# Value tiles of the projections made with an image's first two quarters, and stored ahead of its last quarter's parts

## The chip, the cores and the metric

The kernel runs on one core of a Trainium2 chip. The metric is the device time of one execution in microseconds (us). Besides the timed runs there is one execution recorded by the hardware profiler; all rows below come from it, and its times count from the start of its span.

## The reference, cut to what matters

The program is a small vision tower: four images of 512 tokens by 256 channels go through three attention layers with 16 heads of 16 channels, and through two mixture-of-experts layers. The change touches only the projections at the head of each attention layer: from the layer's input they make queries, keys and values.

```python
# layer "tok" (all tokens, no mask)
qkv = einsum('bysd,ed->byse', x, w_qkv) + b_qkv          # q, k, v: 256 columns each
# layer "rot" (rotary positions, causal)
q = x @ wq_w + wq_b; k = x @ wk_w + wk_b; v = x @ wv_w + wv_b
q = apply_rope(q, pos, ROPE_BASE); k = apply_rope(k, pos, ROPE_BASE)
# layer "top" (causal, the 32 largest scores of a row are kept)
q = x @ Wq.T + bq; k = x @ Wk.T + bk; v = x @ Wv.T + bv
```

In "rot" and "top" a class token stands before the 512 tokens, so keys and values have 513 rows.

## The kernel before

The program is a sequence of stages. Each has its own buffers and semaphores and ends in a barrier of all engines, so that nothing of the next stage starts before the last DMA of this one has landed. The three projection stages are calls of one function, `project` (tags "tok", "rot", "top"); the attention stage that follows each one reads queries, keys and values back from DRAM.

`project` goes through the images b = 0 to 3, and in each through four *quarters* k = 0 to 3. Quarters 0 and 1 make the two halves of the channels of the queries, quarters 2 and 3 those of the keys, each as 128 channels by 512 tokens. With each quarter one *value tile* (128 tokens by 256 channels) is made. In a quarter

- TensorE makes the quarter in `ps` (L288; in "rot" also a swapped version in `ps_rot`, L293), then the value tile k in `ps_v` (L298). Both have two buffers. It waits before a quarter until `full` of the quarter two earlier is out of PSUM, and before a value tile until the tile two earlier was added (`v_ok`).
- VectorE adds the bias and scales, into `full` (L365, in "rot" L352, L355 and L360). Then it calls `split` for the quarter *before* this one: `rest` = `full` - `hi` (L330), and the addition of the bias to the value tile of that earlier quarter, from PSUM into the big buffer `va` (L336). The first such addition of a stage also waits for `v_ones`, that is for GpSimd to have filled `va` with zeros and ones (L401, L403).
- ScalarE rounds `full` to bf16 as `hi` (L388), and after it rounds the earlier quarter's `rest` as `mid` (L381). Before `hi` it waits until the stores of the same quarter of the image before have landed (`stored[k]`), since there is one set of parts for each k.
- GpSimd makes `lo` = `rest` - `mid` (L411).
- SyncE waits for `lo` and issues two DMAs of 192 KB for the quarter (L253). After the fourth quarter of an image it waits for its four value tiles and issues one DMA of 1024 KB (L261; in "top" L257, in rows by position). At the end of the stage it waits for all stores (L266 to L268).

All DMAs here are issued by SyncE, on one queue. After the last image VectorE runs `split` once more, for the last quarter. So the end of a stage is a chain: last `full`, `rest` of quarter 2 and of quarter 3, `mid`, `lo`, the stores, the barrier.

Of the kernel before, what the change touches and what calls it, by code (L numbers as in the profile page):

```python
# [24 lines left out]
ALU = mybir.AluOpType  # L25
# [3 lines left out]
P = 128  # L29
B = 4  # L30
S = 512
D = 256
DC = D // P
NH = 16
HD = D // NH
NQ = S // P
NT = B * NQ
G = 4
HG = NH // G
# [148 lines left out]
def project(c, tag, w, qkb, vb, cls, rope=None):  # L188
# [10 lines left out]
    with c.stage() as st:  # L199
        full = c.sbuf(st, f"{tag}_full", [P, 2, S + 1], F32)  # L200
        rest = c.sbuf(st, f"{tag}_rest", [P, 2, S + 1], F32)
        parts = c.sbuf(st, f"{tag}_parts", [P, SPLIT, 4, S + 1], BF16)
        lo, mid, hi = parts[:, 0], parts[:, 1], parts[:, 2]
        kcls = c.sbuf(st, f"{tag}_kcls", [P, DC, B], F32)
        va = c.sbuf(st, f"{tag}_va", [P, NT, NH, STRIP], F32)
# [7 lines left out]
        ps_v = c.psum(st, f"{tag}_ps_v", [P, 2, S])  # L213
# [7 lines left out]
        hi_ok = c.sem(st, f"{tag}_hi_ok")  # L221
        rest_ok = c.sem(st, f"{tag}_rest_ok")
        mid_ok = c.sem(st, f"{tag}_mid_ok")
        lo_ok = c.sem(st, f"{tag}_lo_ok")
        stored = [c.sem(st, f"{tag}_stored{i}") for i in range(4)]
        v_mm = c.sem(st, f"{tag}_v_mm")
        v_ok = c.sem(st, f"{tag}_v_ok")
        v_ones = c.sem(st, f"{tag}_v_ones")
# [9 lines left out]
        def span(k):  # L238
            return slice(0 if cls and k // 2 == 1 else 1, S + 1)

        @block.sync
        def _(sp):
            for i in range(4):
                sp.sem_inc(stored[i], 16)
            for b in range(B):
                for k in range(4):
                    which, gg = k // 2, k % 2
                    dst = (c.qd, c.kd[S + 1 if cls else S])[which]
                    sp.wait_ge(hi_ok, b * 4 + (k + 1))
                    sp.wait_ge(mid_ok, b * 4 + (k + 1))  # L250
                    sp.wait_ge(lo_ok, 2 + b * 4 + (k + 1))
                    for i in range(2):
                        sp.dma_start(dst[b, 2 * gg + i].rearrange("i d h t -> (d h) i t"),  # L253
                                     parts[i * HD * HG:(i + 1) * HD * HG, :, k, span(k)]).then_inc(stored[k], 16)
                sp.wait_ge(v_ok, 2 + (b + 1) * NQ)
                if by_position:
                    sp.dma_start(c.vp[b, 1:, :].rearrange("(n p) w -> p n w", p=P),  # L257
                                 va[:, b * NQ:b * NQ + NQ, :, :].rearrange("p n h s -> p n (h s)")
                                 ).then_inc(v_out, 16)
                else:  # L260
                    sp.dma_start(c.vd[b], va[:, b * NQ:b * NQ + NQ, :, :].rearrange("p n h s -> p n (h s)")  # L261
                                 ).then_inc(v_out, 16)
            if by_position:
                sp.wait_ge(vc_ok, 1)
                sp.dma_start(c.vp[:, 0, :], vc[:, :, :].rearrange("b h s -> b (h s)")).then_inc(v_out, 16)
            sp.wait_ge(v_out, 16 * (B + 1 if by_position else B))  # L266
            for i in range(4):
                sp.wait_ge(stored[i], 16 + B * step_stores)  # L268

        @block.tensor  # L270
        def _(pe):
            pe.wait_ge(c.fetched, fetched)
            if cls:
                for gg in range(DC):
                    for ch in range(DC):
                        pe.matmul(ps_c[:, 0, gg * B:gg * B + B], w[:, ch, D + gg * P:D + gg * P + P],
                                  c.xt[:, ch, :, 0], start=ch == 0, stop=ch == DC - 1)
                for ch in range(DC):
                    mm = pe.matmul(ps_c[0:B, 1, 0:D], c.xt[:, ch, :, 0], w[:, ch, 2 * D:3 * D],
                                   start=ch == 0, stop=ch == DC - 1)  # L280
                mm.then_inc(cls_mm, 1)

            for b in range(B):
                for k in range(4):
                    which, gg = k // 2, k % 2
                    pe.wait_ge(full_ok, b * 4 + (k + 1))
                    for ch in range(DC):
                        mm = pe.matmul(ps[:, k % 2, :], w[:, ch, which * D + gg * P:which * D + gg * P + P],  # L288
                                       c.xt[:, ch, b, 1:S + 1], start=ch == 0, stop=ch == DC - 1)
                    if rope:  # L290
                        at = (3 + which) * D + gg * P
                        for ch in range(DC):
                            mm = pe.matmul(ps_rot[:, k % 2, :], w[:, ch, at:at + P],  # L293
                                           c.xt[:, ch, b, 1:S + 1], start=ch == 0, stop=ch == DC - 1)
                    mm.then_inc(qk_mm, 1)
                    pe.wait_ge(v_ok, b * NQ + (k + 1))
                    for ch in range(DC):
                        mm = pe.matmul(ps_v[:, k % 2, 0:D], c.xt[:, ch, b, 1 + k * P:1 + k * P + P],  # L298
                                       w[:, ch, 2 * D:3 * D], start=ch == 0, stop=ch == DC - 1)
                    mm.then_inc(v_mm, 1)  # L300

        @block.vector
        def _(dve):
# [21 lines left out]
            def split(b, k):  # L325

                dve.wait_ge(full_ok, b * 4 + (k + 3))
                dve.wait_ge(hi_ok, b * 4 + (k + 1))
                dve.wait_ge(lo_ok, b * 4 + (k + 1))
                dve.tensor_tensor(rest[:, k % 2, span(k)], full[:, k % 2, span(k)], hi[:, k, span(k)],  # L330
                                  ALU.subtract).then_inc(rest_ok, 1)
                n = b * NQ + k
                if isinstance(b, int) and n == 0:
                    dve.wait_ge(v_ones, 2)
                dve.wait_ge(v_mm, n + 1)
                dve.tensor_tensor(va[:, bass.ds(n, 1), :, 0:HD].rearrange("p a h d -> p (a h) d"),  # L336
                                  ps_v[:, k % 2, 0:D].rearrange("p (h d) -> p h d", d=HD),
                                  vb[:, :].rearrange("p (h d) -> p h d", d=HD), ALU.add).then_inc(v_ok, 1)

            def image(b, before):  # L340

                done = 0
                for k in range(4):
                    which, gg = k // 2, k % 2
                    dve.wait_ge(qk_mm, b * 4 + (k + 1))
                    dve.wait_ge(rest_ok, b * 4 + (k + 1))
                    dve.wait_ge(full_ok, b * 4 + (k + 1))
                    if cls and which == 1:
                        dve.tensor_copy(full[:, k % 2, 0:1], kcls[:, gg, bass.ds(b, 1)]).then_inc(turn_ok, 1)
                        done += 1  # L350
                    if rope:
                        dve.scalar_tensor_tensor(out=plain[:, k % 2, :], in0=ps[:, k % 2, :],  # L352
                                                 scalar=qkb[:, gg, which:which + 1], in1=cos[:, which, :],
                                                 op0=ALU.add, op1=ALU.mult).then_inc(turn_ok, 1)
                        dve.scalar_tensor_tensor(out=turned[:, k % 2, :], in0=ps_rot[:, k % 2, :],  # L355
                                                 scalar=qkb[:, gg, 2 + which:3 + which], in1=sin[:, which, :],
                                                 op0=ALU.add, op1=ALU.mult).then_inc(turn_ok, 1)
                        done += turns
                        dve.wait_ge(turn_ok, b * per_image + done)
                        dve.tensor_tensor(full[:, k % 2, 1:], plain[:, k % 2, :], turned[:, k % 2, :],  # L360
                                          ALU.add).then_inc(full_ok, 1)
                    else:
                        if cls and which == 1:
                            dve.wait_ge(turn_ok, b * per_image + done)
                        dve.tensor_scalar(full[:, k % 2, 1:], ps[:, k % 2, :], qkb[:, gg, which:which + 1],  # L365
                                          QSCALE if which == 0 else 1.0, ALU.add, ALU.mult).then_inc(full_ok, 1)
                    if k:
                        split(b, k - 1)
                    elif before:
                        split(b - 1, 3)  # L370

            image(0, False)
            with dve.Fori(1, B) as b:
                image(b, True)
            split(B - 1, 3)

        @block.scalar
# [2030 lines left out]
```

## Time and profile before

| | |
|---|---|
| median of 3 runs | 2251.83 us (2251.66 to 2253.17) |
| profiled execution | 2252.28 us |
| its span | 2250.5 us, 34321 instructions |
| TensorE busy | 1455.1 us (65%) |
| VectorE busy | 1541.9 us (69%) |
| ScalarE / GpSimd busy | 777.0 us (35%) / 429.7 us (19%) |
| projection "tok" | from 17.2 us; the next stage starts at 72.6 us |
| projection "rot" | from 369.1 us; the next stage starts at 456.3 us |
| projection "top" | from 1137.0 us; the next stage starts at 1195.4 us |

The busy shares are averages over stages with different limits. The three projection stages together are about 200 us of the span; what the change does must be read in them.

### The profile page before, as it was taken

The page shows a single profiled execution, that of the slowest core. Times are in us where ns is not written, and L with a number is a line of the kernel's source. Part 1 is how long each engine was busy: PE and PEld are TensorE (multiplying, and loading weights), DVE is VectorE, ACT ScalarE, POOL GpSimd, SP SyncE. Part 2 cuts the span into 40 slices and gives each one's busy share as a digit, 9 for nine tenths or more (in the row PEclk, how much of TensorE's full clock was granted, in tenths as well). Part 3 has the DMA queues.
Part 4 walks back from the last instruction along what each step waited for, and adds up shares of the span by engine and source line. Part 5 has one row for each costly group of instructions (what it writes and reads, how often), then busy time and mean ns, then how long its engine had stood idle before and what let it go on. Part 6 is the DMA issues. An engine that isn't in the chain of part 4 may idle for free. (4 is left out here: it accounts for less than half of the span.)

```text
span 2250.5 us, 34321 instructions
## 1 busy us (share of the span) xinstructions
PE 1455.1 (65%) x10012; PEld 786.0 (35%) x10013; DVE 1541.9 (69%) x4918; ACT 777.0 (35%) x1805; POOL 429.7 (19%) x874
## 2 busy tenths in 40 slices
PE   6588889868887329998093445455454554547992
PEld 3122225434444306665051222232232222324561
DVE  4578867657776401111356999999999999976456
ACT  3256663225554102222042333333333333323330
POOL 4100001200000140000642333333333333320000
PEclk9699999969999659999585555555555555558995
DMA  5472220543325021111343000011100000001001
GB/s 168 147 257 72 73 62 12 149 120 76 75 56 212 35 71 43 45 45 44 91 122 104 20 20 20 20 27 30 21 20 20 20 20 20 20 5 43 0 0 39
DMA packets 93418, 137.52 MB, mean 61 GB/s; under 512 B 9528, under 2 KB 75984, under 8 KB 91480
## 3 DMA queue, kind: packets, MB, share of 16 engines
q1 hardware_dynamic: 90008, 127.38, 19.4%
q0 software_dynamic: 3264, 8.41, 1.2%
q8 instruction: 65, 1.06, 0.2%
q14 instruction: 81, 0.66, 0.1%
HBM read 82.50 MB, written 53.76 MB: 61 GB/s over the span
## 5 line engine op out<-in xcount | busy, mean ns | idle before, releaser
L912 PE MATMUL top_ps_pt<-ident,top_e 128*128 128x128 f32 x640 | 188.6, 428 | 264.7 <-POOL top_e L1027 218.0
L1078 DVE MATCH_REPLACE8 top_left<-top_next,top_left 128x33 f32<-128x33 f32 (+15 forms) x768 | 322.4, 428 | 0.0
L1073 DVE MAX8 top_next<-top_left 128x8 f32<-128x33 f32 (+15 forms) x768 | 301.0, 433 | 0.0
L961 ACT ACTIVATE top_e<-top_ps_s,top_neg_max 128x33 f32<-128x33 f32 (+15 forms) x256 | 124.0, 484 | 424.9 <-POOL top_neg_max L1013 405.0
L1027 POOL TENSOR_TENSOR top_e<-top_e,top_left 128x33 f32<-128x33 f32 (+15 forms) x256 | 191.1, 768 | 368.7 <-DVE top_left L1078 368.2
L912 PEld LDWEIGHTS top_ps_pt<-ident,top_e 128*128 128x128 f32 x640 | 113.0, 212 | 310.7 <-issue 309.3
L684 DVE TENSOR_REDUCE tok_rowmax<-tok_ps_s 128x1 f32<-128x512 f32 x256 | 167.1, 688 | 44.8 <-PE tok_ps_s L527 42.2
L1582 DVE TENSOR_TENSOR moe_hid<-moe_act_gate,moe_ps_h 128x512 f32<-128x512 f32 x39 | 26.8, 688 | 220.2 <-ACT moe_act_gate L1543 220.2
L926 PE MATMUL top_ps_pv<-top_prob_t,top_vs 128*32 128x128 f32 x1280 | 82.9, 421 | 115.7 <-ACT top_prob_t L974 115.7
L684 DVE TENSOR_REDUCE rot_rowmax<-rot_ps_s 128x1 f32<-128x128 f32 (+3 forms) x256 | 115.8, 488 | 47.2 <-PE rot_ps_s L530 43.2
L1482 PE MATMUL moe_ps_h<-moe_w,moe_rows_t 128*128 x312 | 142.5, 600 | 0.4 <-issue 0.4
L657 ACT ACTIVATE tok_et<-tok_ps_st 128x1024 f32<-128x1024 f32 x128 | 124.3, 1021 | 52.3 <-PE tok_ps_st L561 52.3
L527 PE MATMUL tok_ps_s<-tok_ks,tok_qs 96*128 96x512 bf16 x256 | 102.5, 412 | 40.3 <-DMA tok_vs<-v_rows 30.5
L894 PE MATMUL top_ps_s<-top_ks,top_qs 96*32 96x1 bf16 (+15 forms) x1024 | 102.3, 380 | 35.5 <-DMA top_ks<-k_parts 24.9
L657 ACT ACTIVATE rot_et<-rot_ps_st 128x1024 f32<-128x1024 f32 (+3 forms) x128 | 88.0, 703 | 82.8 <-PE rot_ps_st L564 82.8
L1068 DVE MATCH_REPLACE8 top_left<-top_e 128x33 f32<-128x33 f32 (+15 forms) x256 | 108.0, 428 | 0.3 <-issue 0.3
L1060 DVE MAX8 top_raw<-top_ps_s 128x8 f32<-128x33 f32 (+15 forms) x256 | 99.9, 432 | 9.9 <-PE top_ps_s L896 9.9
L974 ACT ACTIVATE top_prob_t<-top_ps_pt 128x128 f32<-128x128 f32 (+3 forms) x256 | 102.7, 430 | 10.2 <-PE top_ps_pt L912 10.2
L926 PEld LDWEIGHTS top_ps_pv<-top_prob_t,top_vs 128*32 128x32 f32 x1280 | 51.1, 162 | 136.1 <-ACT top_prob_t L974 103.4
L1387 POOL DMA_INDIRECT moe_xs<-ctx,row x34 | 33.3, 981 | 329.1 <-issue 329.1
L527 PE MATMUL rot_ps_s<-rot_ks,rot_qs 96*128 96x128 bf16 (+3 forms) x256 | 75.9, 319 | 24.8 <-DVE rot_rowmax L684 23.6
L561 PE MATMUL tok_ps_st<-tok_qs,tok_ks 128*128 128x512 bf16 x256 | 78.9, 391 | 10.4 <-DVE tok_qs L715 8.3
(331 smaller groups left out, 2931.3 us busy)
## 6 DMA issues: line engine op xcount, KB each, us to landing
moe_w<-in_moe_w SPq DMA_DIRECT2D x3, 4096.0 KB, 24.0
moe_xs<-zeros SPq DMA_DIRECT2D x1, 5120.0 KB, 20.7
last_xs<-zeros SPq DMA_DIRECT2D x1, 5120.0 KB, 33.6
moe_rows<-moe_xs SPq DMA_DIRECT2D x40, 128.0 KB
moe_ys<-moe_y SPq DMA_DIRECT2D x38, 128.0 KB, 1.7
v_rows<-tok_va SPq DMA_DIRECT2D x4, 1024.0 KB
tok_vs<-v_rows SPq DMA_DIRECT2D x16, 256.0 KB
v_rows<-rot_va SPq DMA_DIRECT2D x4, 1024.0 KB
```

The lines of the kernel that those rows point to most:

```text
L527: mm = pe.matmul(ps_s[:, u % 2, 0:keys(qt)], lhs, k[0:PARTS * HD, h, k0:k0 + keys(qt)], start=True, stop=not causal)
L657: act.activation(et[:, kt % 2, 2 * pr:2 * pr + 2, q_from(kt):], ps_st[:, 2 * pr:2 * pr + 2, q_from(kt):], ACT.Exp).then_inc(exp_ok, 1)
L684: dve.tensor_reduce(rowmax[:, g % 2, u:u + 1], ps_s[:, u % 2, 0:keys(qt)], AX_X, ALU.max).then_inc(max_ok, 1)
L912: mm = pe.transpose(ps_t[:, U % 2, ch * P:ch * P + P], e[:, U % KEPT, ch * P:ch * P + P], c.ident[:, :])
L926: pe.matmul(ps_pv[lanes, :], v[:, ch, lanes], prob_t[:, n % 2, ch, h, :], start=ch == 0, stop=False)
L961: act.activation(e[:, U % KEPT, 0:keys(U)], row(U), ACT.Exp, bias=neg_max[:, U % 4:U % 4 + 1]).then_inc(e_ok, 1)
L974: act.activation(prob_t[:, n % 2, 0:J + 1, :, QS * (j % 4):QS * (j % 4) + QS], ps_t[:, U % 2, 0:P * (J + 1)].rearrange("p (c h q) -> p c h ...
L1027: pool.tensor_tensor(e[:, U % KEPT, 0:w], e[:, U % KEPT, 0:w], left[:, U % 4, 0:w], ALU.subtract).then_inc(prob_ok, 1)
L1068: dve.match_replace(left[:, U % 4, 0:w], e8[:, U % 4, :], e[:, U % KEPT, 0:w], 0.0).then_inc(pick, 1)
L1073: dve.max(next8[:, U % 2, step // 2, :], left[:, U % 4, 0:keys(U)]).then_inc(pick, 1)
L1078: ins = dve.match_replace(left[:, U % 4, 0:w], next8[:, U % 2, step // 2 - 1, :], left[:, U % 4, 0:w], 0.0)
L1482: mm = pe.matmul(ps_h[:, k % 2, half, :], rows_t[:, k % 2, ch, :], w1[:, ch, bass.ds(e, 1), half * S:half * S + S].rearrange("p a n -> p ( ...
```

## The change

The value tiles are made two at a time with the quarters 0 and 1, and none with the quarters 2 and 3. On VectorE their additions leave `split`; a new function `add_values` makes them right behind `full` of the same quarter, ahead of `split` for the quarter before. SyncE issues the value store of an image after quarter 2's stores and ahead of its waits for quarter 3. Numbers and sizes of matmuls, additions and DMAs stay the same, and all three projections are changed.

```diff
         def _(sp):
+            def store_values(b):
                 sp.wait_ge(v_ok, 2 + (b + 1) * NQ)
...
             for b in range(B):
                 for k in range(4):
                     which, gg = k // 2, k % 2
+                    if k == 3:
+                        store_values(b)
                     dst = (c.qd, c.kd[S + 1 if cls else S])[which]
...
                     mm.then_inc(qk_mm, 1)
-                    pe.wait_ge(v_ok, b * NQ + (k + 1))
-                    for ch in range(DC):
-                        mm = pe.matmul(ps_v[:, k % 2, 0:D], c.xt[:, ch, b, 1 + k * P:1 + k * P + P],
-                                       w[:, ch, 2 * D:3 * D], start=ch == 0, stop=ch == DC - 1)
-                    mm.then_inc(v_mm, 1)
+                    for n in (2 * k, 2 * k + 1) if k < 2 else ():
+                        pe.wait_ge(v_ok, b * NQ + (n + 1))
+                        for ch in range(DC):
+                            mm = pe.matmul(ps_v[:, n % 2, 0:D], c.xt[:, ch, b, 1 + n * P:1 + n * P + P],
+                                           w[:, ch, 2 * D:3 * D], start=ch == 0, stop=ch == DC - 1)
+                        mm.then_inc(v_mm, 1)
...
                                   ALU.subtract).then_inc(rest_ok, 1)
-                n = b * NQ + k
-                if isinstance(b, int) and n == 0:
-                    dve.wait_ge(v_ones, 2)
-                dve.wait_ge(v_mm, n + 1)
-                dve.tensor_tensor(va[:, bass.ds(n, 1), :, 0:HD].rearrange("p a h d -> p (a h) d"),
-                                  ps_v[:, k % 2, 0:D].rearrange("p (h d) -> p h d", d=HD),
-                                  vb[:, :].rearrange("p (h d) -> p h d", d=HD), ALU.add).then_inc(v_ok, 1)
+
+            def add_values(b, k):
+                for n in (2 * k, 2 * k + 1) if k < 2 else ():
+                    if isinstance(b, int) and b == 0 and n == 0:
+                        dve.wait_ge(v_ones, 2)
+                    dve.wait_ge(v_mm, b * NQ + (n + 1))
+                    dve.tensor_tensor(va[:, bass.ds(b * NQ + n, 1), :, 0:HD].rearrange("p a h d -> p (a h) d"),
+                                      ps_v[:, n % 2, 0:D].rearrange("p (h d) -> p h d", d=HD),
+                                      vb[:, :].rearrange("p (h d) -> p h d", d=HD), ALU.add).then_inc(v_ok, 1)
...
+                    add_values(b, k)
                     if k:
                         split(b, k - 1)
                     elif before:
```

## Rows read from the trace of the kernel before

**Rows 1.** Windows of the three projections (us; busy us of each engine, clock, DMA).

```profile
17.40:59.80 42.40, 42.37 (x125) 24.34 (x126) 26.27 (x43) 18.98 (x30) 22.23 (x16) 1.00 0.57 171
372.70:442.50 69.80, 69.80 (x191) 36.64 (x191) 49.22 (x86) 17.67 (x29) 19.45 (x16) 0.98 0.40 119
1140.30:1182.80 42.50, 42.50 (x127) 24.50 (x127) 27.05 (x54) 17.67 (x29) 19.67 (x18) 0.96 0.59 172
```

**Rows 2.** Timeline of the start of "tok" (start us, duration us, engine, line).

```profile
21.13 0.75 DVE L365 TENSOR_SCALAR tok_full<-tok_ps,tok_qkb 128x512 f32<-128x512 f32 x1 [20.99 <-PE tok_ps L288]
...
21.72 1.88 PE L288 MATMUL tok_ps<-xt,tok_w 128*128 128x512 f32 x4
...
23.44 1.03 PE L298 MATMUL tok_ps_v<-tok_w,xt 128*128 128x256 f32 x4
...
24.23 0.56 POOL L403 MEMSET tok_va<- 128x256 f32 x1
24.30 1.88 PE L288 MATMUL tok_ps<-xt,tok_w 128*128 128x512 f32 x4
24.31 0.68 DVE L330 TENSOR_TENSOR tok_rest<-tok_full,tok_parts 128x512 f32<-128x512 f32 x1
...
24.91 0.42 DVE L336 TENSOR_TENSOR tok_va<-tok_ps_v,tok_vb 128x256 f32<-128x256 f32 x1
```

**Rows 3.** Timeline of the end of "tok", to the next stage's first DMA.

```profile
59.54 1.16 POOL L411 TENSOR_TENSOR tok_parts<-tok_rest,tok_parts 128x512 bf16<-128x512 f32 x1 [1.28 <-ACT tok_parts L381]
...
59.84 0.75 DVE L365 TENSOR_SCALAR tok_full<-tok_ps,tok_qkb 128x512 f32<-128x512 f32 x1 [0.70 <-PE tok_ps L288]
60.50 0.74 DVE L330 TENSOR_TENSOR tok_rest<-tok_full,tok_parts 128x512 f32<-128x512 f32 x1
...
61.99 2.17 POOL L411 TENSOR_TENSOR tok_parts<-tok_rest,tok_parts 128x512 bf16<-128x512 f32 x2 [1.29 <-ACT tok_parts L381]
...
63.21 2.59 SPq L253 DMA_DIRECT2D k_parts<-tok_parts  x4
65.84 0.68 SPq L261 DMA_DIRECT2D v_rows<-tok_va  x1
...
72.58 1.26 SPq L182 DMA_DIRECT2D tok_qs<-q_parts  x3
```

**Rows 4.** Windows of 1 us at the end of "tok" (last columns: DMA share, GB/s).

```profile
65.00:66.00 1.00, 0.00 (x0) 0.00 (x0) 0.00 (x0) 0.00 (x0) 0.00 (x0) 0.55 0.84 223
...
69.00:70.00 1.00, 0.00 (x0) 0.00 (x0) 0.00 (x0) 0.00 (x0) 0.00 (x0) 0.50 0.99 418
70.00:71.00 1.00, 0.00 (x0) 0.00 (x0) 0.00 (x0) 0.00 (x0) 0.00 (x0) 0.50 0.30 123
```

**Rows 5.** Timeline: SyncE's last key stores of "rot" and of "top".

```profile
447.25 2.57 SPq L253 DMA_DIRECT2D k_parts<-rot_parts  x4
...
1186.34 2.90 SPq L253 DMA_DIRECT2D k_parts<-top_parts  x4
```

**Rows 6.** Windows: the last microsecond with DMA data of "rot" and of "top".

```profile
454.00:455.00 1.00, 0.00 (x0) 0.00 (x0) 0.00 (x0) 0.00 (x0) 0.00 (x0) 0.50 0.38 156
...
1193.00:1194.00 1.00, 0.00 (x0) 0.00 (x0) 0.00 (x0) 0.00 (x0) 0.00 (x0) 0.50 0.73 279
```

**Rows 7.** Timeline of "tok" where VectorE's rest meets GpSimd's lo.

```profile
44.61 1.08 POOL L411 TENSOR_TENSOR tok_parts<-tok_rest,tok_parts 128x512 bf16<-128x512 f32 x1 [2.31 <-ACT tok_parts L381]
...
44.95 1.29 DVE L330 TENSOR_TENSOR tok_rest<-tok_full,tok_parts 128x512 f32<-128x512 f32 x1
```

**Rows 8.** Timeline of the starts of "rot" and of "top": GpSimd's last fill of va, VectorE's first full.

```profile
376.09 0.69 POOL L403 MEMSET rot_va<- 128x256 f32 x1
...
1144.01 0.54 POOL L403 MEMSET top_va<- 128x256 f32 x1
...
1145.45 0.73 DVE L365 TENSOR_SCALAR top_full<-top_ps,top_qkb 128x512 f32<-128x512 f32 x1
```

**Rows 9.** Waits of ScalarE in "tok" (us in total, times, longest).

```profile
ACT tok_parts L388 <- DMA q_parts<-tok_parts: 3.9, 2, 2.2
```

More of the change, by code:

```diff
@@ L242, in _ @@
         def _(sp):
[L243 to L254, printed above, removed]
+            def store_values(b):
                 sp.wait_ge(v_ok, 2 + (b + 1) * NQ)
@@ L262, in _ @@
                                  ).then_inc(v_out, 16)
+            for i in range(4):
+                sp.sem_inc(stored[i], 16)
+            for b in range(B):
+                for k in range(4):
+                    which, gg = k // 2, k % 2
+                    if k == 3:
+                        store_values(b)
+                    dst = (c.qd, c.kd[S + 1 if cls else S])[which]
+                    sp.wait_ge(hi_ok, b * 4 + (k + 1))
+                    sp.wait_ge(mid_ok, b * 4 + (k + 1))
+                    sp.wait_ge(lo_ok, 2 + b * 4 + (k + 1))
+                    for i in range(2):
+                        sp.dma_start(dst[b, 2 * gg + i].rearrange("i d h t -> (d h) i t"),
+                                     parts[i * HD * HG:(i + 1) * HD * HG, :, k, span(k)]).then_inc(stored[k], 16)
             if by_position:
```

## The prediction

> **What bounds the kernel now.** I read the table of instructions for the three projection stages first, then one window over each stage from its first projection matmul to the end of its last quarter, then the timeline of each start and end, and at last windows of 1 us over the ends.
>
> The windows say that TensorE sets the pace: it is busy 42.37 of 42.40 us in "tok", 69.80 of 69.80 in "rot" and 42.50 of 42.50 in "top" [rows 1]. VectorE has 26 to 49 us in the same stretches. TensorE's numbers repeat: the four matmuls of a quarter take 1.72 us (21.72 to 23.44), the four of a value tile 0.86 us (23.44 to 24.30) [rows 2]. A quarter with its tile takes 2.58 us, and from the first `full` at 21.13 to the last at 59.84 there are 15 x 2.58 = 38.7 us [rows 2, 3]: nothing is lost, although ScalarE waits twice for a store [rows 9].
>
> The second part of a stage is its tail, which no matmul is in. In "tok" the last `full` starts at 59.84; GpSimd's last two `lo` run from 61.99 to 64.16; SyncE issues four key stores from 63.21 and the value store at 65.84; the next stage's first DMA is at 72.58 [rows 3]. In between the DMA engines are the bound: share 0.84 at 223 GB/s while they carry keys, 0.99 at 418 GB/s while they carry values, and in the microsecond from 70.0 the share is 0.30, so that data end at about 70.3 [rows 4]. That is a sum of bytes: four stores of 192 KB are 0.79 MB, at 223 GB/s 3.5 us; the values are 1.05 MB, at 418 GB/s 2.5 us; with about 1.1 us from the issue to the first data it makes 7.1 us from 63.21. The same distance, key issue to end of data, is 454.38 - 447.25 = 7.1 us in "rot" and 1193.73 - 1186.34 = 7.4 us in "top" [rows 5, 6] (shares 0.38 and 0.73 of the last microsecond). So three tails of about 7 us hang on one moment: the issue of quarter 2's stores.
>
> **The change part by part.**
>
> *Work in total.* Matmuls, additions, DMAs and bytes keep their number. No term comes from counts.
>
> *TensorE's order.* The last tile used to be made after the last quarter, where only its addition and the late value store needed it. Now all tiles are made before quarter 2, so TensorE does 0.86 us more before the last quarter is complete. As TensorE is without a gap up to there [rows 1], the last `full` of each stage is 0.86 us later. Everything in the tail starts from it: `rest` of quarter 2 stands behind it on VectorE, and `mid`, `lo` and the key stores behind that. Three stages: 3 x 0.86 = +2.6 us. Bounds: 0, if the tail hung on something else, and 0.86 in each; I take 0.86.
>
> *SyncE's order.* The value store is issued after quarter 2's two stores, still behind the same `lo`. In "tok" it goes out some 1.3 us (two issues of 0.65) after the first key store, so at 64.5 on the old clock against 65.84 before, but what follows it is the last quarter's 0.39 MB. The engines drain the same 1.84 MB from the same first issue; only the order differs. Bounds: -0.4 us a stage if the engines' share of 0.84 to 0.9 during the keys rises to 0.99 by the mix, +0.3 if the last, small stores leave some engines idle; I take 0. The two last key stores are issued behind the value issue of 0.68 us, well before the queue runs dry.
>
> *The addition's new place.* In the first image the addition now stands directly behind the first `full`, and it must wait for `v_ones`. In "tok" GpSimd's last fill ends at 24.23 + 0.56 = 24.79, and the first addition ran at 24.91, where it had `full` of quarter 1 and a `rest` before it [rows 2]. Now VectorE is through with its first `full` at 21.88 and stands still until about 24.85; the addition ends at about 25.27. Behind it queue the second addition, `full` of quarter 1 and the first `rest`. Who waits for that: TensorE may not write its third tile before the first was added. Its first tile ends at 21.72, where quarter 1 now starts; then come the second tile and quarter 1, 0.86 + 1.72 us, so it is ready for the third at 24.30 and can start at 25.4 to 25.6. That is a gap of 1.0 to 1.4 us in an engine that has none; it is not won back in the stage. I take +1.2. In "rot" the fill ends at 376.78, and the first quarter (eight matmuls from 372.70, 3.44 us at full clock, then three VectorE passes of some 0.7 us) can't be ready for an addition before 378; in "top" at 1144.55, before the first `full` at 1145.45 [rows 1, 8]. There the wait costs 0; in "top" TensorE reaches its third tile at about 1147.2, after the additions.
>
> *Later images.* The quarters 0 and 1 now take 3.44 us of TensorE in "tok" and "top", 2 and 3 take 1.72. VectorE needs in a short quarter 0.75 + 0.68 = 1.43, ScalarE 18.98 / 15 = 1.3, GpSimd 1.16: all below 1.72 [rows 1 to 3]. In a long one VectorE has 2 x 0.42 more against 1.72 more. `stored[k]`: quarter 0's store now comes about 8.4 us after its `full` instead of 5.9, as its `rest` stands behind a long quarter 1, and ScalarE will wait for it some 1 us in the next image; the value store ahead of quarter 3's makes that one land late too. Both waits end in a long quarter, where the `rest` that needs this `hi` is over 2.5 us away. Bounds: 0, and 1 us an image in two stages; I take 0, since the waits of up to 2.2 us that stand there now cost TensorE nothing [rows 9, 1].
>
> *Two engines on one memory.* A `rest` that starts at 44.95 while `lo` runs from 44.61 to 45.69 takes 1.29 us instead of 0.68 [rows 2]: it ends 0.55 us after `lo`, as if it had started then [rows 7]. In the old tail `lo` of quarter 1 (59.54 to 60.70) only grazes `rest` of quarter 2 (60.50, 0.74 us) [rows 3]. With short quarters `rest` of quarter 2 comes 0.86 us closer to it and lies over it, in "tok" and "top"; in "rot" a short quarter still has 3.44 us, and they stay apart. Bounds for each of the two: 0, if `rest` comes first, and 1.1 us, if it waits out a whole `lo`; I take 0.5 in "tok", where both are due within 0.1 us, and 0.75 in "top", where the copy of the class token puts `rest` later. +1.25 us. (The Trainium skill, GPSIMD Engine Reference, section 1, Specifications, says that GpSimd shares its SBUF interfaces with VectorE and that instructions with two SBUF inputs contend. By it alone the sum is the same; it is why I expect this of `rest` and not of the additions, which read one operand from PSUM.)
>
> Sum: 2.6 + 0 + 1.2 + 0 + 1.25 = +5.0 us. On the profiled execution, 2252.28 (span 2250.5), it makes 2257.3. That execution is 0.45 us above the median of the runs; on the median 2251.83 it makes 2256.8 us, +0.22%.
>
> **The rivals.**
>
> *A, only the shift (and the gap).* `rest` and `lo` don't meet, because `rest` is first: 2.6 + 1.2 = +3.8, or +2.6 if TensorE's gap is hidden too: 2254.4 to 2255.6. For it: neither engine's order in the tail is forced. Against it: [rows 7] and the spacing.
>
> *B, the last store's own time decides.* If a stage ends with its last store's own latency and not with the bytes of all, a small store behind the big one is cheap: the value store goes out at 64.5 + 0.86 = 65.4 instead of 65.84, and all ends 0.45 us earlier; three times, with the gap of 1.2, -0.2 us: 2251.7. For it: the landing wait is what the barrier sees. Against it: the DMA share near 0.9 before that. (The Trainium skill, DMA: Bandwidth & Descriptors, section Anatomy of one DMA, gives a DMA about 2.0 us plus its bytes at 436 GB/s. As an estimate from that page the old value store, issued at 65.84, would end at 70.2, which agrees with the trace's 70.3; but by it the key stores would be done at about 68, and that the trace doesn't bear out: they flow at 223 GB/s.)
>
> *C, faster.* If the values are drained in the tail's quiet part, before the last `lo`, a stage ends 2.5 us (their transfer) earlier and 0.86 later: 3 x -1.64 + 1.2 = -3.7 us, and with nothing lost at the start -4.9: 2247 to 2248. It decides if the store gets out 2.5 us or more before quarter 3's. For it: the tiles are complete before quarter 2. Against it: SyncE issues in order, behind the stores of quarter 2, and the two last `lo` are 1.09 us apart [rows 3].
>
> *D, TensorE loses its pace.* If one of the waits for `stored[k]` or `rest` reaches a short quarter, it costs about 1 us an image in "tok" and "top": 6 more, 2263.
>
> **How the numbers follow.** Forecast 0.45 (own range 2255.5 to 2258.5); A 0.28; B 0.12; C 0.07; D 0.08. About 4.5 us, 0.2%, is what a measurement of this kernel can tell from no change, and the forecast lies just beyond it. Slower: D, two thirds of the forecast's chance and part of A by unknown sizes of the gap, 0.48. Faster: C, 0.07. Same: 0.45. The range 2252.8 to 2259.5 leaves out C, most of B and D.
>
> **What would show it.** Right: the last `full` of "tok" near 61.9 (0.86 + 1.2 later than 59.84), of "rot" and "top" 0.86 us later from their stage's start; a gap in TensorE near 24.3 to 25.5; the window over "rot" still without a gap; the distance from quarter 2's store to the end of data again 7.1 to 7.4 us; a `rest` of over 1 us in the tails of "tok" and "top". Wrong: a distance clearly under 7 us (B or C), TensorE under 99% busy in the later images (D), or no gap at the start of "tok".

## The result, and the profile after

| | before | after |
|---|---|---|
| median of 9 runs | 2251.83 us (2250.28 to 2255.90) | 2258.99 us (2256.59 to 2264.12) |
| ratio | | 1.0031, 95% interval 1.0020 to 1.0041 |
| profiled execution, span | 2252.28, 2250.5 us | 2258.16, 2256.4 us |

The change makes the kernel 7.2 us slower; 5.0 were forecast. The lines of the changed file stand some lines lower: `full` is L372, `rest` L335, `hi` L396, `lo` L419, the matmuls L292 and L303, the stores L265 (parts) and L250 or L246 (values).

Each stage is divided below at four moments that can be read in the timelines: TensorE's first matmul of quarter 0 in the first image (the class token's small matmuls before it are left out), VectorE's last `full`, SyncE's first store of quarter 2 in the last image, and the first DMA of the next stage. The last stretch, from that store to the next stage, is called the drain.

| us | before tok / rot / top | after tok / rot / top |
|---|---|---|
| first matmul to last `full` | 42.4 / 71.3 / 42.7 | 44.7 / 72.1 / 44.6 |
| last `full` to quarter 2's store | 3.4 / 3.3 / 3.3 | 5.3 / 3.2 / 6.2 |
| that store to the next stage | 9.4 / 9.0 / 9.0 | 9.0 / 9.3 / 9.8 |
| whole stage, from GpSimd's fill | 55.3 / 87.2 / 58.4 | 59.2 / 88.3 / 62.5 |

The three stages together go from 200.85 to 209.97 us, +9.1. A second trace of each kernel gives 200.84 and 209.89: the sums repeat to 0.1 us, single stages to 0.2. Inside "top" after, the second trace divides differently, 6.6 us to the store and 9.3 in the drain, with the same total. The remainder of the span does not repeat: 2049.65 and 2049.56 us before, 2046.43 and 2050.41 after, of which the attention stage between "tok" and "rot" alone has 294.96 and 299.38. So +9.1 is the change's effect where it acts; what lies between it and the 7.2 of the medians is in stages whose code is the same.

The end of "tok" after, which answers to [rows 3] (timeline: start, duration, engine, line):

```profile
58.21 3.60 PE L292 MATMUL tok_ps<-xt,tok_w 128*128 128x512 f32 x8
...
60.79 1.19 DVE L335 TENSOR_TENSOR tok_rest<-tok_full,tok_parts 128x512 f32<-128x512 f32 x1
...
62.21 0.75 DVE L372 TENSOR_SCALAR tok_full<-tok_ps,tok_qkb 128x512 f32<-128x512 f32 x1 [0.23 <-issue]
62.73 1.16 POOL L419 TENSOR_TENSOR tok_parts<-tok_rest,tok_parts 128x512 bf16<-128x512 f32 x1 [1.28 <-ACT tok_parts L389]
62.88 1.55 DVE L335 TENSOR_TENSOR tok_rest<-tok_full,tok_parts 128x512 f32<-128x512 f32 x1
65.06 0.63 ACT L396 ACTIVATE tok_parts<-tok_full 128x512 bf16<-128x512 f32 x1 [2.41 <-DMA k_parts<-tok_parts]
65.60 0.62 ACT L389 ACTIVATE tok_parts<-tok_rest 128x512 bf16<-128x512 f32 x1
65.78 0.69 DVE L335 TENSOR_TENSOR tok_rest<-tok_full,tok_parts 128x512 f32<-128x512 f32 x1 [1.35 <-ACT tok_parts L396]
66.29 2.17 POOL L419 TENSOR_TENSOR tok_parts<-tok_rest,tok_parts 128x512 bf16<-128x512 f32 x2 [2.41 <-ACT tok_parts L389]
...
67.50 1.23 SPq L265 DMA_DIRECT2D k_parts<-tok_parts  x2
68.78 0.60 SPq L250 DMA_DIRECT2D v_rows<-tok_va  x1
69.48 2.13 SPq L265 DMA_DIRECT2D k_parts<-tok_parts  x2
76.51 3.54 POOL L521 MEMSET tok_ks<- 32x2048 bf16 x2 [8.05 <-POOLq L92]
76.52 1.25 SPq L182 DMA_DIRECT2D tok_qs<-q_parts  x3
```

Three things are new here. The last `full` no longer starts with the end of TensorE's matmuls (59.80 and 59.84 before) but 0.4 us behind it (61.81 and 62.21), 0.2 us after the end of a `rest` that took 1.19 us; that the semaphore of this `rest` is what it waited for is read from the order of the code. `rest` of quarter 2 (62.88) takes 1.55 us, since GpSimd's `lo` began at 62.73. And the last `hi` should follow the last `full`, whose 0.75 us end at 62.96, but it starts at 65.06: ScalarE waits for a key store. It is the store of quarter 3 of the *previous* image, which shares its buffer; in the new order it stands behind that image's 1 MB of values. `mid` of quarter 2 is queued behind this `hi` on ScalarE (65.60), so even quarter 2's store, whose own `rest` was done at 64.4, is held up. SyncE's stores of the previous image show the order:

```profile
57.87 0.61 SPq L265 DMA_DIRECT2D k_parts<-tok_parts  x1
...
58.53 0.60 SPq L250 DMA_DIRECT2D v_rows<-tok_va  x1
...
59.23 2.15 SPq L265 DMA_DIRECT2D k_parts<-tok_parts  x2
```

In "top" it is longer (`hi` starts 3.7 us after the last `full` starts); in "rot", with its longer quarters, it doesn't occur. Timelines of the ends of "top" and "rot", which answer to [rows 5]:

```profile
1184.57 0.75 DVE L372 TENSOR_SCALAR top_full<-top_ps,top_qkb 128x512 f32<-128x512 f32 x1
1185.17 1.16 POOL L419 TENSOR_TENSOR top_parts<-top_rest,top_parts 128x512 bf16<-128x512 f32 x1 [1.53 <-ACT top_parts L389]
1185.23 1.65 DVE L335 TENSOR_TENSOR top_rest<-top_full,top_parts 128x513 f32<-128x513 f32 x1
1188.28 0.63 ACT L396 ACTIVATE top_parts<-top_full 128x513 bf16<-128x513 f32 x1 [3.18 <-DMA k_parts<-top_parts]
...
1190.74 1.23 SPq L265 DMA_DIRECT2D k_parts<-top_parts  x2
...
1200.52 1.25 SPq L182 DMA_DIRECT2D top_qs<-q_parts  x3
```

```profile
447.97 0.63 ACT L396 ACTIVATE rot_parts<-rot_full 128x513 bf16<-128x513 f32 x1 [2.22 <-DVE rot_full L367]
...
450.46 1.23 SPq L265 DMA_DIRECT2D k_parts<-rot_parts  x2
...
459.77 1.26 SPq L182 DMA_DIRECT2D rot_qs<-q_parts  x3
```

ScalarE's idle time in "tok" after that the landing of a store ended (in total, times, longest); before, only the second kind was there, 3.9 us in 2 [rows 9]:

```profile
ACT tok_parts L396 <- DMA k_parts<-tok_parts: 8.4, 5, 2.4
...
ACT tok_parts L396 <- DMA q_parts<-tok_parts: 2.7, 4, 1.0
```

The drain itself, in windows of 1 us (last columns: DMA share, GB/s), answers to [rows 4]: the order inside it changed, the time from quarter 2's store to the end of data hardly. Data now flow from 68.8 to 74.5, the values in the middle at 412 to 434 GB/s; from 67.50 that is 7.0 us against 7.1. By the same reading it is 7.0 against 7.1 in "rot" and 7.15 against 7.4 in "top". What grew in those two is the time from the end of data to the next stage: 1.9 to 2.3 us in "rot", 1.7 to 2.6 in "top" (2.1 in the second trace). Why is not shown.

```profile
70.00:71.00 1.00, 0.00 (x0) 0.00 (x0) 0.00 (x0) 0.00 (x0) 0.00 (x0) 0.50 1.09 335
71.00:72.00 1.00, 0.00 (x0) 0.00 (x0) 0.00 (x0) 0.00 (x0) 0.00 (x0) 0.50 1.04 434
72.00:73.00 1.00, 0.00 (x0) 0.00 (x0) 0.00 (x0) 0.00 (x0) 0.00 (x0) 0.50 1.05 412
73.00:74.00 1.00, 0.00 (x0) 0.00 (x0) 0.00 (x0) 0.00 (x0) 0.00 (x0) 0.50 0.81 237
74.00:75.00 1.00, 0.00 (x0) 0.00 (x0) 0.00 (x0) 0.00 (x0) 0.00 (x0) 0.50 0.47 163
```

The start of "tok", to be held against [rows 2]. TensorE's clock is read here from the matmuls' own durations, since the profile's clock column shows 1.00 from the start: a matmul of 512 columns takes 0.86 us in the first quarter and 0.43 later. First the trace shown so far. Its eight matmuls of the first two tiles take 2.75 us (21.05 to 23.80), so that TensorE came to its full clock (2.4 GHz, from 1.2) only during them, at about 23. Then the second trace of the same kernel, where the same eight take 1.72 us, all at the full clock, as the first tile before did:

```profile
21.05 2.92 PE L303 MATMUL tok_ps_v<-tok_w,xt 128*128 128x256 f32 x8
...
23.80 1.88 PE L292 MATMUL tok_ps<-xt,tok_w 128*128 128x512 f32 x4
...
24.86 0.75 DVE L343 TENSOR_TENSOR tok_va<-tok_ps_v,tok_vb 128x256 f32<-128x256 f32 x2 [2.75 <-POOL tok_va L411]
25.52 1.89 PE L303 MATMUL tok_ps_v<-tok_w,xt 128*128 128x256 f32 x8
```

```profile
21.02 1.89 PE L303 MATMUL tok_ps_v<-tok_w,xt 128*128 128x256 f32 x8
22.74 1.88 PE L292 MATMUL tok_ps<-xt,tok_w 128*128 128x512 f32 x4
25.44 2.00 PE L303 MATMUL tok_ps_v<-tok_w,xt 128*128 128x256 f32 x8 [0.82 <-DVE tok_va L343]
```

### The profile page after: what moved, and what is told of

It reads as the page before. It is cut to its first block and busy times, and to the rows that moved or that the text cites. A ratio compares the mean times of both kernels' runs of the same rounds, so it can differ in the third digit from the quotient of the medians.

```text
span 2256.4 us, 34289 instructions
## 1 busy us (share of the span) xinstructions
PE 1443.5 (64%) x9980; PEld 783.9 (35%) x10013; DVE 1551.1 (69%) x4918; ACT 777.3 (34%) x1805; POOL 431.6 (19%) x874
## 5 line engine op out<-in xcount | busy, mean ns | idle before, releaser
L535 PE MATMUL tok_ps_s<-tok_ks,tok_qs 96*128 96x512 bf16 x256 | 102.1, 410 | 42.7 <-DMA tok_vs<-v_rows 32.9
L1021 POOL TENSOR_SCALAR top_neg_max<-top_raw 128x1 f32<-128x1 f32 x256 | 52.9, 212 | 171.6 <-DVE top_raw L1068 169.1
```

Of the source, the lines that this page charges most:

```text
L535: mm = pe.matmul(ps_s[:, u % 2, 0:keys(qt)], lhs, k[0:PARTS * HD, h, k0:k0 + keys(qt)], start=True, stop=not causal)
```

## The experiments

Each median is compared with runs of the kernel before on the same chip, whose medians were 2252.1 to 2253.5 us; between experiments the ratios are what can be compared. The table at the end of this section has the numbers of all of them.

**The value store last again.** `store_values(b)` is called after the loop over k; tiles stay in pairs.

```diff
-                    if k == 3:
-                        store_values(b)
...
+                store_values(b)
```

> The changed kernel, but each image's value store is issued after quarter 3's stores, as before. Theory 1 (the value store ahead of quarter 3's makes that store land late, and in the last image ScalarE's hi of quarter 3 waits for it on the path of the tail): the distance from the last full to quarter 2's store falls from 5.3 us (tok) and 6.2 us (top) to 3.3 to 3.8 us in both, and 3.5 to 4.7 us go from the changed kernel's time: about 2254.5. Theory 2 (the tails are longer because rest and lo meet in the short quarters): that distance stays above 5 us, the time near 2259.

Measured: 2258.02 us, ratio 1.0021 (1.0011 to 1.0031). The distance from the last `full` to quarter 2's store is 4.1 in "tok" and 4.0 in "top", from 5.3 and 6.2. The last `hi` follows the last `full` at once in "tok":

```profile
62.20 0.75 DVE L371 TENSOR_SCALAR tok_full<-tok_ps,tok_qkb 128x512 f32<-128x512 f32 x1 [0.23 <-issue]
62.71 1.16 POOL L418 TENSOR_TENSOR tok_parts<-tok_rest,tok_parts 128x512 bf16<-128x512 f32 x1 [1.28 <-ACT tok_parts L388]
62.87 2.15 DVE L334 TENSOR_TENSOR tok_rest<-tok_full,tok_parts 128x512 f32<-128x512 f32 x2
62.98 0.63 ACT L395 ACTIVATE tok_parts<-tok_full 128x512 bf16<-128x512 f32 x1 [0.35 <-DVE tok_full L371]
```

So the late store is worth 1.2 + 2.2 = 3.4 us of path at that place, and it was made by the store's order. The whole came down less: the stages' sum only from 210.0 to 208.25. In "tok" the drain behind is 9.5 us instead of 9.0. In "top" the last `full` comes 1.3 us later: 0.6 because TensorE was done later, having started with the slower clock, and 0.7 because VectorE was behind it. TensorE's last matmuls end at 1186.05 there, but the last `full` starts at 1187.37, after a `rest` of twice its usual time:

```profile
1185.57 1.41 DVE L334 TENSOR_TENSOR top_rest<-top_full,top_parts 128x512 f32<-128x512 f32 x1
...
1187.37 0.75 DVE L371 TENSOR_SCALAR top_full<-top_ps,top_qkb 128x512 f32<-128x512 f32 x1
```

The median came down by 1 us instead of the 3.5 to 4.7 expected, and its interval overlaps the changed kernel's, so the medians do not show the gain. And 4.1 is not 3.4: theory 2 holds for a part, the two `rest` of the last image's end in "tok" take 2.15 us together.

**Two sets of parts.** `parts` and `stored` get 8 places, b % 2 * 4 + k, and the images are unrolled on VectorE, ScalarE and GpSimd.

```diff
-                    act.wait_ge(stored[k], b * step_stores + 16)
+                    act.wait_ge(stored[b % 2 * 4 + k], b // 2 * step_stores + 16)
```

> The changed kernel with two sets of parts (even and odd images), so that hi waits for the stores of two images earlier; the order of the stores stays the changed kernel's; the images are unrolled. Theory 1: ScalarE waits for no store, last full to quarter 2's store is 3.3 to 4 us in tok and top, and the time 2254 to 2256. Theory 2: the distance stays above 5 us and the time within 1 us of the changed kernel's.

Measured: 2259.54 us, 1.0032 (1.0020 to 1.0044). ScalarE waits for no store in any projection, and the distance is 3.8 and 4.1 us in the changed kernel's own order of stores: the buffer's reuse was the wait. The stages' sum is 206.9, 3.1 below the changed kernel's 210.0. The time did not follow (2254 to 2256 had been expected): the remainder of the span was 2050.6 us in its trace, against 2046.4 and 2050.4 in the changed kernel's two. So the wait and its price are shown in the stages, by this run and the one before, and not in the medians.

**The first image's part of `va` filled first.** The fill is cut at image 1; VectorE waits for the second part before its loop.

```diff
-            pool.memset(va[:, :, :, :], 0.0).then_inc(v_ones, 1)
+            pool.memset(va[:, 0:NQ, :, :], 0.0).then_inc(v_ones, 1)
```

> The changed kernel, but GpSimd fills the first image's part of va first (a quarter of the 6.9 us) and lets the first addition go; the rest is filled behind. If the fill made TensorE's gap at the start of tok (and of top), the third value tile follows quarter 1 at once there and the last full of tok comes 1.0 to 1.4 us earlier, of top about 1 us: 2 us off, 2257. If the gap is no part of the path (the clock or the late stores decide), the time stays near 2259.

Measured: 2262.13 us, 1.0042 (1.0029 to 1.0056): no gain in the median. In "tok" the third tile starts at 24.98, right behind quarter 1 (from 23.27), and the first matmul to the last `full` takes 44.2 instead of 44.7; in "top" 43.9 instead of 44.6, though the whole of "top" was no shorter (63.0 us against 62.5; its first matmuls ran at the slower clock). In "tok" the eight matmuls of the first two tiles take 2.22 us, so the clock was late here too and TensorE with it: the fill's gap and the late clock lie over each other, and only one of them is paid.

**The value store first.** `if k == 3` becomes `if k == 0`: an image's values go out ahead of its quarter 0's stores, when its four tiles are ready anyway.

> The changed kernel, but the value store of an image is issued ahead of quarter 0's stores instead of quarter 3's. Theory 1 with a tail that is a sum of bytes: the values (2.5 us of DMA) leave the tail, so quarter 2's store to the next stage falls from 9.0 to 9.3 us to some 6.5 to 7.5 in all three stages, and quarter 3's parts have nothing large ahead of them: last full to quarter 2's store 3.3 to 4. Time 2246 to 2251, below the kernel before. Rival: in tok and top the DMA engines are full, so that the waits only move to another quarter and the tail stays: 2255 or more, with a gain in rot alone (2 us).

Measured: 2249.23 us, 0.9986 (0.9977 to 0.9995): faster than the kernel before, and 0.45%, 10 us, below the changed kernel, which differs from it in one digit of the source. Quarter 2's store to the next stage falls to 6.5, 6.4 and 6.8 us: the 2.5 us of the values are out of all three tails, and before the last `hi` only the short wait in "top" is left, as with the values last. SyncE in the last image of "tok":

```profile
59.67 0.60 SPq L250 DMA_DIRECT2D v_rows<-tok_va  x1
61.52 3.67 SPq L265 DMA_DIRECT2D q_parts<-tok_parts  x4
66.33 2.58 SPq L265 DMA_DIRECT2D k_parts<-tok_parts  x4
72.82 1.25 SPq L182 DMA_DIRECT2D tok_qs<-q_parts  x3
```

**Both together**, the value store first and the early fill.

> The changed kernel with the value store ahead of quarter 0's stores, and GpSimd filling the first image's part of va first. Both together. If the fill costs what TensorE's gap would be at a full clock (1.0 to 1.4 us in tok, 1 in top), it is 1 to 2 us below the kernel with the value store first: 2247 to 2248. Rival: the early fill bought nothing in the changed kernel (2262.1 against 2259.0), so it costs something elsewhere and here too: 2249 to 2252.

Measured: 2247.48 us, 0.9974 (0.9964 to 0.9985), the fastest here. Its stages are 199.6 us, no less than the 198.9 with the store first alone, with the clock late again in "tok". So that the fill adds something is not shown; its interval touches the other's.

**The early fill in the kernel before.** The same edit of the fill there.

> The kernel before with the early fill alone. In tok the fill is no wait there and in top VectorE's first full waits for the filled vc, so the start of top may gain up to 1.5 us on VectorE that TensorE does not need. Theory (the early fill is harmless): 2250 to 2252.5. Rival (it is harmful by itself, as the changed kernel with it was 3 us slower): 2254 to 2256.

Measured: 2253.66 us, 1.000 (0.999 to 1.001): harmless by itself. Nor is it shown to harm the changed kernel, since the two intervals there overlap. This trace had 2057.1 us outside the projections, against 2049.6 in the kernel before.

**The value store ahead of quarter 2's**: `if k == 2`.

> The changed kernel with the value store ahead of quarter 2's stores instead of quarter 3's. Theory 1 (a store behind the values lands late, and what it holds up in the last image is on the tail): now quarter 2's and 3's stores are both behind it; rot, whose DMA engines have room, gets the short tail (quarter 2's store to the next stage 6.4 us as with the values first), while tok and top keep a wait of hi in the tail (last full to quarter 2's store over 4.5) but lose the values' 2.5 us from the rest of it. Time 2252 to 2255, between the changed kernel and the one with the values first. Rival (only the bytes in the tail count): as with the values first, 2249.

Measured: 2258.25 us, 1.0019 (1.0010 to 1.0029). The time missed the expected 2252 to 2255. The mechanism came as expected (last `full` to quarter 2's store 5.2 and 5.9 in "tok" and "top", 3.2 in "rot"), the size not: the drain is 8.6, 7.6 and 9.0 us, so it got shorter in "rot" alone by over 1 us. With the values directly ahead of the last two quarters' keys their bytes are still in the drain: in "tok" they flow at 420 to 427 GB/s from 69 to 71 us, behind quarter 2's store at 67.66.

**A short `lo`.** As the first experiment, with `lo` of the last image's quarter 1 on 8 columns.

```diff
+                    cols = slice(1, 9) if k == short else span(k)
```

> As the changed kernel with the value store last, but in the last image GpSimd's lo of quarter 1 covers 8 columns instead of 512 (that part of the keys' and queries' parts is left out). Theory: rest of quarter 2 is slowed because it meets this lo; so it takes 0.7 us, and last full to quarter 2's store falls from 4.1 and 4.0 us (tok, top) to 3.3 to 3.5. Rival: the short quarters themselves or ScalarE's order hold the chain, and the distance stays at 4.0.

Measured in a single execution (2259.86 us): the distance is 3.26 us in "tok" and 3.65 in "top". The row to compare is `rest` of quarter 2, directly behind the short `lo`:

```profile
62.84 0.21 POOL L419 TENSOR_TENSOR tok_parts<-tok_rest,tok_parts 128x8 bf16<-128x8 f32 x1 [1.28 <-ACT tok_parts L388]
62.99 0.68 DVE L334 TENSOR_TENSOR tok_rest<-tok_full,tok_parts 128x512 f32<-128x512 f32 x1
```

It takes 0.68 us instead of 1.46 (2.15 less the second one's 0.69). The meeting of the two engines is worth 0.9 us in "tok"; in "top" `rest` is 0.6 us shorter and the distance 0.35, as `hi` still starts 0.2 us after `full` there, behind a store. (The Trainium skill, GPSIMD Engine Reference, section 1, Specifications, says that the two engines share their SBUF interfaces, with contention for instructions with two SBUF inputs; this run agrees.)

**The last image in the old order.** As the first experiment, but in image 3 one tile a quarter.

```diff
+                    for n in (k,) if b == B - 1 else (2 * k, 2 * k + 1) if k < 2 else ():
```

> As the changed kernel with the value store last, but the last image makes its value tiles one a quarter, as before; the images 0 to 2 keep the pairs. Theory (the tail hangs on the last full, which the pairs put 0.86 us later, and on rest meeting lo in the short quarters): against the kernel with the value store last, the last full comes 0.86 us earlier from the first matmul in all three stages, last full to quarter 2's store falls from 4.1 and 4.0 us to 3.4, and what is left over the kernel before is the start alone (up to 1.4 us in tok): 2252 to 2255. Rival (the pairs cost in every image): the last full stays where it is, 2258.

Measured: 2257.50 us, 1.0016 (1.0007 to 1.0025). From the first matmul to the last `full` the stage "rot" takes 71.2 instead of 72.2 and "tok" 43.4 instead of 44.9: the shift is there and goes with the last image's order (in "tok" it is more than 0.86, since VectorE is no longer behind TensorE at the last `full`). But "top" keeps 44.6, as TensorE waits 1.0 us for an addition in the last image there, and the distance to quarter 2's store is 4.5 in both: where pairs are followed by single tiles the last image reaches its buffers earlier than the image before has stored them, and `hi` waits again (ScalarE is idle for 1.27 and 1.72 us). The expectation of 3.4 us, and with it the time, was wrong.

**The two kernels once more**, for the clock.

> The kernel before once more, for the moment at which TensorE's granted clock rises in tok (20.1 us in its first trace). If that moment is a matter of chance, it lies anywhere up to some 3 us around; if it goes with the program, near 20 again. Time 2250 to 2256.

> The changed kernel once more. If the clock's moment is chance, it may rise near 20 here, and then the gap in TensorE before the third value tile shows (1.0 to 1.4 us); if it goes with the program, it rises near 22 again and there is no gap. Last full to quarter 2's store 5.3 and 6.2 us in tok and top as in the first trace. Time 2256 to 2262.

Measured: 2252.20 and 2262.05 us. In both TensorE is at its full clock by the first value tile (20.78 and 21.02 us). With that TensorE's gap in the changed kernel shows, from the end of quarter 1 (22.74 + 1.72 = 24.46) to 25.44, 1.0 us. The third tile starts at 25.4 to 25.5 in both traces of the changed kernel, whatever the clock did. (The expectations put the clock's rise in the first traces at 20.1 and 22 us; worked out from the durations it is 20.7 and 23.1.) The moment differs between two executions of one program, 23.1 and 20.9 us. But in the other eight traces with paired tiles it lies between 22.1 and 23.7 and in the three without at 20.4 to 20.7, so whether the order of the work has a part in it stays open.

| kernel | us, ratio to before | last `full` to store, tok / top | store to next, tok / rot / top | three stages |
|---|---|---|---|---|
| before | 2251.83 | 3.4 / 3.3 | 9.4 / 9.0 / 9.0 | 200.85 |
| changed | 2258.99, 1.0031 | 5.3 / 6.2 | 9.0 / 9.3 / 9.8 | 209.97 |
| values last | 2258.02, 1.0021 | 4.1 / 4.0 | 9.5 / 9.1 / 9.7 | 208.25 |
| two sets | 2259.54, 1.0032 | 3.8 / 4.1 | 10.1 / 9.1 / 9.5 | 206.92 |
| early fill | 2262.13, 1.0042 | 5.2 / 6.1 | 8.5 / 8.9 / 9.4 | 208.90 |
| values first | 2249.23, 0.9986 | 4.1 / 4.0 | 6.5 / 6.4 / 6.8 | 198.92 |
| values first, early fill | 2247.48, 0.9974 | 4.1 / 4.0 | 6.2 / 6.7 / 7.1 | 199.56 |
| before, early fill | 2253.66, 1.0000 | 3.4 / 3.3 | 9.2 / 9.0 / 9.2 | 200.71 |
| values third | 2258.25, 1.0019 | 5.2 / 5.9 | 8.6 / 7.6 / 9.0 | 208.01 |
| last image old | 2257.50, 1.0016 | 4.5 / 4.5 | 9.7 / 9.1 / 9.8 | 205.80 |
| short `lo` (one execution) | 2259.86 | 3.3 / 3.7 | 9.2 / 9.1 / 9.7 | 207.10 |
| before, again (one execution) | 2252.20 | 3.4 / 3.3 | 9.2 / 9.1 / 9.2 | 200.84 |
| changed, again (one execution) | 2262.05 | 5.2 / 6.6 | 9.1 / 9.3 / 9.3 | 209.89 |

## Why the prediction was right, and which step failed

The sign, the place (three tails and a start) and most steps were right; one step failed and cost 3.4 us more, and others were off by less than 1 us. That the time still came out inside the range, 2252.8 to 2259.5, is partly luck: the 9.1 us of the stages alone, on the median before, make 2260.9. Of the rivals, A's 3.8 us leave out the meeting of `rest` and `lo`, which the short `lo` shows; the shorter stages of B and C are not there.

- *TensorE's order, +0.86 a stage*: right. "rot", which has nothing else, is 0.9 us later at the last `full` (74.88 to 75.76 from the stage's start) and 1.1 in all.
- *SyncE's order, 0*: right for the bytes. The order inside the drain doesn't matter to them, quarter 2's store to the end of data is 7.0 to 7.15 us. The drain as a whole, to the next stage, is 0.35 us shorter in "tok" and 0.3 and 0.7 longer in "rot" and "top". The note under rival B is off in two places. The section Anatomy of one DMA, in DMA: Bandwidth & Descriptors of the Trainium skill, gives its fit for DMAs issued from GpSimd, and those here are SyncE's. And its "about 68" for the end of the key stores does agree with the trace as the prediction reads it: 63.21 + 1.1 + 3.5 is 67.8. Neither enters the sum. That the drain is a sum of bytes is why the idea of the change, values out of the tail, gave nothing where it was put and 2.5 us a stage where the store came early enough (rival C's mechanism, with the store at quarter 0).
- *The gap at the start, +1.2 in "tok", 0 in "top"*: in "tok" right as a bound, third tile at 25.5 (25.4 to 25.6 were named). In "top" wrong: there TensorE waited 0.85 us for the first addition (row below). I had taken TensorE's start from a trace in which its first matmuls ran at half clock; GpSimd's fill doesn't get faster with the clock (6.92 us in "tok" and 6.93 in "top" in all traces that have it whole), so a faster start only ran into it. (In "top" the first addition stands behind the first `full`, and that behind a copy that waits for the fill of `vc`, at 1146.28.) Together with the shift it makes the last `full` of "top" 0.5 us later from the fill, where 0.86 were forecast.

```profile
1147.61 1.99 PE L303 MATMUL top_ps_v<-top_w,xt 128*128 128x256 f32 x8 [0.85 <-DVE top_va L343]
```

- *`rest` and `lo`, +0.5 and +0.75*: right, 0.8 and 0.7 by the kernel with the values last against the one before, 0.9 in "tok" by the short `lo`.
- *Later images, engines, 0*: TensorE kept its pace, but the claim that VectorE's 1.43 us fit into a short quarter's 1.72 left out the prediction's own term of `rest` meeting `lo`. With a `rest` of 1.2 to 1.4 us they don't fit, and the last `full` starts later behind TensorE's end than before: by 0.4 us in "tok", by 0.2 in "top", and by 1.0 in "top" with the values last.
- *Later images, `stored[k]`, 0*: this step failed. I wrote that both waits end in a long quarter, where the `rest` that needs this `hi` is over 2.5 us away. That holds for the images 1 and 2 and for a quarter 3 that a long quarter follows. After the last quarter 3 of the stage none follows: `rest` is wanted at once, and `mid` of quarter 2 stands behind the waiting `hi`. Measured 1.2 us in "tok" and 2.2 in "top". It is rival D's mechanism, a wait for `stored[k]` in a short quarter, but it cost once, in the tail, and not TensorE's pace image by image.

In the stages, up to the last `full` 3.7 us were added where 3.8 were forecast (2.3 in "tok", 0.9 in "rot", 0.5 in "top"). From there to quarter 2's store it was 4.7 where 1.25 were forecast: 1.4 from `rest` and `lo`, 3.4 from the late store. The drain has 0.7 where 0 was forecast. Together that is 9.1 against 5.0. Why the medians differ by only 7.2 stays open: outside the projections single traces lie from 2046.4 to 2057.1 us, and no run here ties that to the change.

## What to carry to other kernels

- A wait that is harmless in a steady loop must be looked at again in the last iteration: the slack that hides it is often the next iteration's work. Ask of every reused buffer what its wait holds up when nothing follows.
- A tail that is a sum of bytes gets shorter only if bytes leave it. Moving a large store by one place inside the tail costs what it delays; moving it to where the queue has room, here from quarter 3 to quarter 0, turned +0.31% into -0.14%.
- Where one stage is what a change acts on, its length in two traces (to 0.2 us here) tells more than runs of the whole that scatter by 5 to 8 us.

## What had not been expected

- A large store holds up the small one that is issued next to it, and through its buffer a computing engine one image later: 1 MB ahead of two stores of 192 KB left ScalarE idle for 2.4 and 3.2 us.
- The same idle 1 us of TensorE shows in one trace and not in another, with the same program: where the full clock of 2.4 GHz is there by 21.0 us it waits, where it comes at about 23 it is busy at 1.2 GHz instead, and the third value tile starts at 25.4 to 25.5 in both.
